# Expert feed-forward on one core: the weights become the stationary operand of the inner products, and the next tile's expert number is read ahead of the outer products

## What is computed

```
for _ in range(LOOPS):                      # 2
    z_norm = _rmsnorm(z, norm_w)
    logits = z_norm @ router_w
    scores = softmax(logits); topk_vals, topk_idx = top_k(scores, 2)
    topk_vals = topk_vals / (sum(topk_vals) + EPS)
    for e in range(E):                      # 8
        h = silu(flat_z @ w1[e]) * (flat_z @ w3[e])
        mixed = mixed + flat_cw[:, e:e + 1] * (h @ w2[e])
    z = z + mixed.reshape(B, S, D)
```

## Time and profile before

| what | value |
|---|---|
| median of three runs | 1051.33 us |
| the profiled execution | 1050.72 us, its span 1049.0 us |
| granted TensorE clock, mean | 0.989 |
| PE busy | 94% of the span |
| DVE, ACT, POOL busy | 66%, 55%, 55% |
| experts' stage | about 350 to 1028 us of the span |

### The profile page before, as it was taken

How to read it: one execution, slowest core, us unless ns; L and a number is a source line. 1 busy time by engine, 2 the same in 40 slices (tenths; PEclk the granted TensorE clock), 3 DMA queues, 4 the chain that set the end, 5 groups by cost and what they waited for, 6 DMA issues and landing times.

```text
span 1049.0 us, 22711 instructions
## 1 busy us (share of the span) xinstructions
PE 987.4 (94%) x7246; PEld 678.7 (65%) x7246; DVE 690.5 (66%) x1497; ACT 574.7 (55%) x1122; POOL 579.5 (55%) x755
## 2 busy tenths in 40 slices
PE   7999997989999899999999999999999999999991
PEld 5677776668888577665666765666755566666661
DVE  7889987999999454684435557535469433575557
ACT  4578786668888545433335565335574333333333
POOL 3356686866798755444443366443365544455435
PEclk9999999999999999999999999999999999999996
DMA  9921111000000234334346435338434433665573
GB/s 315 370 68 31 38 32 22 1 6 21 15 26 16 67 107 125 87 69 101 91 109 167 132 98 139 88 106 181 112 111 117 96 91 92 170 173 119 143 187 130
DMA packets 153818, 109.26 MB, mean 104 GB/s; under 512 B 100992, under 2 KB 140544, under 8 KB 153728
## 3 DMA queue, kind: packets, MB, share of 16 engines
q1 hardware_dynamic: 140096, 70.82, 26.5%
q0 software_dynamic: 13632, 37.24, 12.0%
HBM read 54.27 MB, written 31.20 MB: 81 GB/s over the span
## 4 chain that ended last, share of the span: by engine, by line
PE 69%; DVE 9%; POOL 7%; DMA 6%; ACT 4%; issue 3%; SPq 0%; another core or an unknown queue 0%; POOLq 0%; ACTq 0%; DVEq 0%
PE psum_s L930 32%; PE psum_o L2336 16%; PE psum_s L2325 6%; DMA arena<-arena 4%; PE psum_s L1758 3%; PE psum_t L1753 2%; PE psum_t L764 2%; PE psum_o L1804 2%; POOL arena L1057 2%; DVE arena L1489 1%; DMA arena<-in_rope 1%; PE psum_o L1799 1%; PE psum_o L1811 1%; PE psum_s L1735 1%; PE psum_t L2300 1%
## 5 line engine op out<-in xcount | busy, mean ns | idle before, releaser
L930 PE MATMUL psum_s<-w_all,arena 128*128 x1704 | 392.0, 380 | 4.6 <-issue 1.9
L1980 POOL DMA_INDIRECT token_rows<-arena,result_row_of_row x142 | 147.1, 1036 | 296.5 <-ACT arena L2089 291.2
L930 PEld LDWEIGHTS psum_s<-w_all,arena 128*128 128x128 f16 x1704 | 157.8, 98 | 185.2 <-issue 10.9
L2336 PE MATMUL psum_o<-w_all,arena 128*128 x1704 | 209.4, 273 | 9.1 <-DVE arena L2264 8.2
L915 DVE SCALAR_TENSOR_TENSOR arena<-psum_s,gate_scale,arena 128x512 f32<-128x512 f32 x142 | 106.5, 750 | 161.1 <-ACT arena L909 80.6
L2336 PEld LDWEIGHTS psum_o<-w_all,arena 128*128 128x128 f16 x1704 | 164.7, 98 | 54.1 <-issue 15.4
L2264 DVE TENSOR_TENSOR arena<-psum_s,arena 128x512 f16<-128x512 f32 x142 | 97.8, 689 | 132.3 <-ACT arena L2082 114.2
L2089 ACT ACTIVATE arena<-psum_o 128x256 f32<-128x256 f32 x142 | 54.3, 383 | 216.8 <-PE psum_o L2336 214.1
L891 POOL DMA_INDIRECT arena<-sorted_rows,token_of_row x142 | 139.9, 986 | 49.3 <-issue 40.2
L909 ACT ACTIVATE arena<-psum_s,silu_scale 128x512 f32<-128x512 f32 x142 | 97.6, 687 | 108.1 <-PE psum_s L930 56.6
L2082 ACT ACTIVATE arena<-psum_s 128x512 f16<-128x512 f32 x142 | 84.7, 597 | 33.1 <-PE psum_s L2325 22.9
(11 more groups left out here) (326 smaller groups left out, 1364.8 us busy)
## 6 DMA issues: line engine op xcount, KB each, us to landing
arena<-token_rows SPq DMA_DIRECT2D x64, 256.0 KB, 3.1
w_all<-in_L_ffn_w SPq DMA_DIRECT2D x24, 512.0 KB, 10.1
sorted_rows<-w_all SPq DMA_DIRECT2D x24, 256.0 KB
out<-x_sb SPq DMA_DIRECT2D x7, 512.0 KB, 3.1
arena<-arena SPq DMA_TRANSPOSE x172, 2.4
arena<-sorted_rows,token_of_row POOLq DMA_INDIRECT x142
token_rows<-arena,result_row_of_row POOLq DMA_INDIRECT x142
x_sb<-in_L_attn_x SPq DMA_DIRECT2D x1, 2048.0 KB, 14.8
```

Of the source, the lines that this page charges most:

```text
L930: last = nc.tensor.matmul(bank, e_xT[:, u, lx * DC + c, :], w_split[:, bass.ds(e * EW + at, FF)], start=(q == 0), stop=(q == 3 * DC - 1))
L1980: nc.gpsimd.indirect_dma_start(rows, bass.IndirectOffsetOnAxis(ap=targets[:, at : at + 1], axis=0), y_row[:, u, :], None).then_inc(s_sent[ ...
L2336: last = nc.tensor.matmul(psum_e, hT[:, lh, c, :], w_split[:, bass.ds(e * EW + at, D)], start=(q == 0), stop=(q == 3 * FC - 1))
```

## The change

Four things, all in the experts' stage:

1. `inner` exchanges the operands. The weights are stationary (blocks of 128x128, at a place held in a register) and the token rows move (128 columns). For each m there are now 4 blocks f of the hidden values times 6 products: 24 matmuls of 128 columns for each m, 48 for a tile. The result has the hidden values on the partitions, so `turn_h` and its semaphore are gone; `h_row` is now `h_all`, already turned, and `h_hi` and `h_lo` read it from SBUF instead of `psum_h`.
2. The addresses are worked out ahead of the matmuls: `place` adds a constant to a multiple of the expert's number, in bytes, once for each place (16 places for each m of `inner`, 8 for `outer`), and the operands use the registers as they are.
3. The waits: `inner(n, e, 0)` waits for `silu(n-1)`, `inner(n, e, 1)` for `gate(n-1)`, which `turn_h` did for both. `gate` waits on its own engine for `h_lo` of the tile before.
4. The number of the next tile's expert is read behind `beside` and ahead of `outer(n-1)`; at the end of a pass the wait for the next pass's numbers stands there too.

```diff
+        W_BASE, LAST_COLUMN = 16512, 2 * (P - 1)
...
+        w_bytes = w_all[:, :].bitcast(mybir.dt.uint8)
...
+            if s:
+                dve.wait_ge(s_h_lo, s)
-            nc.vector.scalar_tensor_tensor(h_row, psum_b, gate_scale[:, 0:1], silu_a, ALU.mult,
+            nc.vector.scalar_tensor_tensor(h_all, psum_b, gate_scale[:, 0:1], silu_a, ALU.mult,
...
+        def place(pe, e, at):
+            r = pe.alloc_register()
+            pe.reg_alu(r, e * (2 * EW), 2 * at + W_BASE, ALU.add)
+            return pe.snap(r, donate=True, min_val=2 * at + W_BASE, max_val=2 * at + W_BASE + 2 * EW * (NE - 1),
+                           guaranteed_mod_val=0, out_of_modulus=2)
+
+        def stationary(r):
+            return w_bytes[:, bass.ds(r - (W_BASE + LAST_COLUMN), 2 * P)].bitcast(F16)
+
+        def moving(r):
+            return w_bytes[:, bass.ds(r - W_BASE, 2 * D)].bitcast(F16)
+
         def inner(pe, n, e, m):
             u = n % UNROLL
+            places = [[place(pe, e, ((m * DC + c) * 2 + lw) * GROUP + f * P + P - 1) for c in range(DC) for lw in range(2)] for f in range(FC)]
             if m == 0:
                 pe.wait_ge(s_turned[u], 16 * (n // UNROLL + 1))
+                if n:
+                    pe.wait_ge(s_silu, n)
+            elif n:
+                pe.wait_ge(s_h, n)
...
-                last = nc.tensor.matmul(bank, e_xT[:, u, lx * DC + c, :], w_split[:, bass.ds(e * EW + at, FF)],
-                                        start=(q == 0), stop=(q == 3 * DC - 1))
+            for f in range(FC):
+                for q, (c, lx, lw) in enumerate([(c, a, w) for c in range(DC) for a, w in ((0, 0), (1, 0), (0, 1))]):
+                    last = nc.tensor.matmul(bank[:, f * P : (f + 1) * P], stationary(places[f][2 * c + lw]),
+                                            e_xT[:, u, lx * DC + c, :], start=(q == 0), stop=(q == 3 * DC - 1))
...
-                act.wait_ge(s_th, s + 1)
-                nc.scalar.activation(hT[:, 0, :, :].rearrange("p c t -> p (c t)"), psum_h, ACT.Copy).then_inc(s_h_hi, 1)
+                act.wait_ge(s_h, s + 1)
+                nc.scalar.activation(hT[:, 0, :, :].rearrange("p c t -> p (c t)"), h_all, ACT.Copy).then_inc(s_h_hi, 1)
...
-                nc.vector.tensor_tensor(hT[:, 1, :, :].rearrange("p c t -> p (c t)"), psum_h,
+                nc.vector.tensor_tensor(hT[:, 1, :, :].rearrange("p c t -> p (c t)"), h_all,
...
-            def turn_h(n):
...
             def outer(n, e):
+                per = GROUP // D
+                places = [[place(pe, e, ((2 * DC + c // per) * 2 + lw) * GROUP + c % per * D) for lw in range(2)] for c in range(FC)]
                 pe.wait_ge(s_h_lo, n + 1)
...
-            before_e = None
+            before_e, e = None, expert(pe, 0, 0)
...
-                    if n:
-                        turn_h(n - 1)
-                    e = expert(pe, k, t)
                     for m in range(2 if n else 0):
                         inner(pe, n, e, m)
                     if k < END:
                         beside(k, plan, t)
+                    next_e = None
+                    if t + 1 < PASS[k]:
+                        next_e = expert(pe, k, t + 1)
+                    elif n + 1 < ALL:
+                        pe.wait_ge(s_eid, k + 2)
+                        next_e = expert(pe, k + 1, 0)
                     if n:
                         outer(n - 1, before_e)
```

More of the change, by code:

```diff
@@ L796, in sandwich_kernel @@
         silu_a = take(FF)
-        h_row = take(FF)
+        h_all = take(FF)
         hT = take(2 * FF // 2).bitcast(F16).rearrange("p (l c t) -> p l c t", l=2, c=FC)
@@ L815, in sandwich_kernel @@
         psum_a, psum_b = psum_s[:, 0:FF], psum_s[:, 512 : 512 + FF]
-        psum_h = psum_s[:, 1024:1536]
         psum_e = psum_o[:, 0:D]
@@ L827, in sandwich_kernel @@
         s_h = sem("h_ready")
-        s_th = sem("h_turned")
         s_h_hi = sem("hT_hi")
@@ L920, in expert @@
             return pe.value_load(expert_of[0:1, at : at + 1], min_val=0, max_val=NE - 1)
+        def place(pe, e, at):
[7 more added lines that the diff above has]
+            return w_bytes[:, bass.ds(r - W_BASE, 2 * D)].bitcast(F16)
         def inner(pe, n, e, m):
             u = n % UNROLL
+            places = [[place(pe, e, ((m * DC + c) * 2 + lw) * GROUP + f * P + P - 1) for c in range(DC) for lw in range(2)] for f in range(FC)]
             if m == 0:
                 pe.wait_ge(s_turned[u], 16 * (n // UNROLL + 1))
+                if n:
+                    pe.wait_ge(s_silu, n)
+            elif n:
+                pe.wait_ge(s_h, n)
             bank, signal = ((psum_a, s_a), (psum_b, s_b))[m]
-            for q, (c, lx, lw) in enumerate([(c, a, w) for c in range(DC) for a, w in ((0, 0), (1, 0), (0, 1))]):
-                at = ((m * DC + c) * 2 + lw) * GROUP
-                last = nc.tensor.matmul(bank, e_xT[:, u, lx * DC + c, :], w_split[:, bass.ds(e * EW + at, FF)],
-                                        start=(q == 0), stop=(q == 3 * DC - 1))
+            for f in range(FC):
+                for q, (c, lx, lw) in enumerate([(c, a, w) for c in range(DC) for a, w in ((0, 0), (1, 0), (0, 1))]):
+                    last = nc.tensor.matmul(bank[:, f * P : (f + 1) * P], stationary(places[f][2 * c + lw]),
+                                            e_xT[:, u, lx * DC + c, :], start=(q == 0), stop=(q == 3 * DC - 1))
             last.then_inc(signal, 1)
@@ L2333, in outer @@
                 for q, (c, lh, lw) in enumerate([(c, a, w) for c in range(FC) for a, w in ((0, 0), (1, 0), (0, 1))]):
-                    per = GROUP // D
-                    at = ((2 * DC + c // per) * 2 + lw) * GROUP + c % per * D
-                    last = nc.tensor.matmul(psum_e, hT[:, lh, c, :], w_split[:, bass.ds(e * EW + at, D)],
+                    last = nc.tensor.matmul(psum_e, hT[:, lh, c, :], moving(places[c][lw]),
                                             start=(q == 0), stop=(q == 3 * FC - 1))
                 last.then_inc(s_e, 1)
-            before_e = None
+            before_e, e = None, expert(pe, 0, 0)
             for k, plan in enumerate(plans):
-                pe.wait_ge(s_eid, k + 1)
                 for t in range(PASS[k]):
                     n = FIRST[k] + t
-                    if n:
-                        turn_h(n - 1)
-                    e = expert(pe, k, t)
                     for m in range(2 if n else 0):
@@ L2355, in _ @@
                         beside_end(k, plan, t)
-                    before_e = e
-            turn_h(ALL - 1)
+                    before_e, e = e, next_e
             outer(ALL - 1, before_e)
```

## The result

The changed kernel took 1038.48 us (median of 4 runs, 1037.29 to 1039.50) against 1052.28 for the kernel before beside it; the ratio is 0.987, 95% interval 0.985 to 0.990. It is faster by 13.8 us. The time lies inside the range, but the gain is half of the 28 us forecast.

What follows compares the result with a forecast made beforehand. Plain tiles were taken as bound by what the PE array streams. Gains of 8.6 (24 tiles), 22 (92 plain tiles) and 0.6 (last tile), less 3 for neighbours, gave -28 us: 1051.3 to 1023 us, range 1006 to 1043.

Steps and rivals of the forecast that it cites:

- where PE waits for others: Step on tiles where PE idles for h_lo: about 14 late tiles gain nothing, neighbours lose 3 us, last tile saves 0.6.
- 24 tiles x 0.36 = 8.6: Term for the tiles with L2300 beside them: each gains the array's whole 0.36 us, 8.6 us together.
- The array: PE's streaming in a tile: transposes save 0.44 us, 48 inner matmuls at 56 ns cost 0.08 more; 4.35 becomes 3.99.
- every rival with a dearer load: Register-addressed weight loads take longer on the array; at 64 ns the gain is gone, 1051 to 1060 us; chance 0.04.
- the stall of 0.12 us: PE's sequencer in 92 plain tiles: takes 0.12 us off each tile's 0.36 gain, with a gap ahead of the outer products.
- which the sum counts at 0: Term for 12 tiles, together with about 14 late for h_lo: no gain in any of them.
- The load's new place: Expert-number load moved ahead of outer(n-1): passes only PE's queue; y_copy and the sending DMA have over 2 us to spare.
- `h_hi` from SBUF: h_hi on ScalarE reads SBUF instead of PSUM: counted as costing nothing, 0 to 0.03 us either way.
- Instruction fetch: PE's longer program: 33 more queue packets at 0.2 us stall would cost 7 us, giving 1030, inside the range.
- neighbours with 3 us in all: Tiles near the late ones, with nearly no slack, become late for h_lo: a loss of 3 us in all.
- still fits: Stretch from 906 to 941 us: VectorE's 3.6 us a tile is under the new tile's 3.99 us.
- VectorE and ScalarE become the bound: Rival: slack shrinks everywhere; routing tiles and those with L2300 or L662 gain nothing, 14 us gained, 1037; chance 0.13.

Runs made afterwards that it cites:

- e3: Changed kernel with every tile using expert 0's weights at fixed addresses, without number loads or register operations: 1024.75 us, ratio 0.974.
- f4: Changed kernel with both the fetch waiting for the second half of inner and expert 0 at fixed addresses: 1011.51 us, ratio 0.963.
- e2: Changed kernel with the expert's number read at the start of its own tile again, in front of inner: 1037.00 us, ratio 0.986.
- e1: Changed kernel with GpSimd waiting for the signal of inner's second half before issuing the fetch: 1024.51 us, ratio 0.976.
- g1: Kernel before with each 512-column inner matmul cut into four of 128, fixed addresses at expert 0: 1101.30 us (one run).
- e4: Kernel before with two small memsets on GpSimd ahead of each fetch, so it starts closer to inner's end: 1052.68 us, ratio 1.002.
- g3: Changed kernel with each fetch a plain transfer of 128 consecutive rows, issued at the same place, instead of an indirect one: 1012.39 us (one run).

## Why the prediction was right and wrong

The forecast had 28 us to gain and the change gave 13.8. What failed is the step on where PE waits for others, and with it the term "24 tiles x 0.36 = 8.6".

*The array: right.* 48 inner matmuls take 2.84 us with the tail of the last (220 ns by L949, of which 56 count): 2.68, as forecast. Register addresses cost the array nothing there: in e3, with fixed ones, the 48 take the same 2.84 us. At 56 ns a pair every rival with a dearer load is out. Of tiles 25 to 42 (72.5 us) one took 4.37 us, and the others 4.01 in the mean.

*The sequencer in plain tiles: the stall of 0.12 us was mostly not there.* It was my estimate, and no run shows it, nor how many operations one FUSED_REGOPS does. With fixed addresses (e3) a plain tile takes 3.99 us, with registers 3.99 to 4.07. Yet fixed addresses were worth 12 to 14 us of the whole (e3 and f4), about what the prediction had given the sequencer (92 x 0.12 = 11). A plain tile has only 0.02 to 0.03 us of that, so most of it lies elsewhere: this term was near by luck. The additions pass in eight FUSED_REGOPS a tile (1136 in 142 tiles), of 42 to 88 ns each, where the forecast has 8 with up to 85:

```profile
L926 PEldq FUSED_REGOPS  x1136: 42/74/88, 350.6 to 1009.6; - x190
```

In one plain tile after (500.95 to 503.29 us) the two ahead of the outer products pass in 0.17 us, the three ahead of m = 0 in 0.38 and the three ahead of m = 1 in 0.34, together 0.89; before, the eight of `outer` took 0.94 (from 500.64) and the eight of `inner` 0.93 (from 503.34), with pairs between them.

In the tiles with L664, which the sum counts at 0, registers cost about 0.3 us: 4.44 to 4.50 us against 4.19 in e3. That took nearly the whole gain there; before, one took 4.54 us (its outer products start at 662.30, the next ones at 666.84). With so little of the stall in plain tiles, the first group gained 0.33 us each where I had 0.24 for most of them.

*The load's new place*: nothing, by e2. *`h_hi` from SBUF*: 626 ns in the mean (L2101) against 597 from PSUM before (L2082), within the 0.03 us of the forecast. *Instruction fetch*: 88 packets, 32 more, but in the regular tiles from 480 to 560 us PE is idle for only 0.5 us.

*Where PE waits for others: this step failed.* It charged neighbours with 3 us in all, gave the 24 tiles with L2300 their whole 0.36 us, and said of the stretch from 906 to 941 us that 3.6 us of VectorE a tile "still fits". All that took for granted that VectorE and ScalarE learn of b and a when these are done, as they do in these tiles before. After, VectorE learns of b some 0.95 us later. In a plain tile that costs nothing: `h_lo` ends at 523.87 + 0.69 = 524.56, 3.1 us after b ended, as forecast, since `h_hi` stands behind `y_copy` anyway. But VectorE's free time between gate and `h_lo` is 0.70 us instead of the 1.51 of e1, and where routing or statistics must fit into it, they don't. The same eight tiles after and in e1 (us, busy PE, PEld, DVE, ACT, POOL, clock, DMA, GB/s):

```profile
896.64:932.14 35.50, 33.24 (x484) 30.85 (x481) 28.71 (x65) 12.88 (x24) 17.58 (x16) 1.00 0.76 179
```

```profile
880.43:912.80 32.37, 32.19 (x483) 30.87 (x481) 28.73 (x69) 12.72 (x24) 17.15 (x16) 1.00 0.93 197
```

VectorE's work is 28.7 us in both, as before. With the signal late it does not fit (35.50 us), with the signal on time it does (32.37, the forecast 3.99 a tile plus 0.06). The argument was sound and its input was not.

The 24 tiles with L2300 (L2319 after) took 133.2 us before and 132.8 after, a gain of 0.4 us where the sum has 8.6. In e1 they took 125.3, a gain of 7.9. Here it is chiefly a, to ScalarE, that is late, with L766 waiting for it; e1 frees a and b together, so the share of each is not measured. This is the largest single miss of the sum.

The size nearly closes: the forecast gain was 28 us, the change gave 13.8, and with the one wait of e1 it is 26.2. That it closes so well is partly luck: the first group gained more than I gave it, and the 33 routing tiles lost 1 us even in e1, where I had at most 14 of them at nothing and the others gaining.

*The rivals.* "VectorE and ScalarE become the bound" (1037) came closest to the time. Its place was right, its reason only in part. In the routing tiles it holds in part: PE's wait for `h_lo` rose from 8.2 to 22.1 us and stays at 22.5 in e1, and even there they take 163.1 us against 162.1 before, so the shorter tile took their slack. In the tiles with L2300 and in those of the statistics it was the late signals.

*What in the profile of before could have warned.* GpSimd issues an indirect transfer for 0.97 us of each tile shortly before b ends. And the effect itself is there, in a few tiles: at the end of the first pass GpSimd issued four indirect transfers in a row, and a, with matmuls of 512 columns, ended at 471.45 + 5 x 0.216 + 0.38 = 472.91 while `silu` started 1.74 us later.

```profile
468.79 0.98 POOL L891 DMA_INDIRECT arena<-sorted_rows,token_of_row  x1 [0.30 <-issue]
...
470.07 0.97 POOL L891 DMA_INDIRECT arena<-sorted_rows,token_of_row  x1 [0.30 <-issue]
...
471.35 0.95 POOL L891 DMA_INDIRECT arena<-sorted_rows,token_of_row  x1 [0.30 <-issue]
...
471.45 2.76 PE L930 MATMUL psum_s<-w_all,arena 128*128 x12
...
472.60 0.99 POOL L1980 DMA_INDIRECT token_rows<-arena,result_row_of_row  x1 [0.30 <-issue]
...
474.65 0.69 ACT L909 ACTIVATE arena<-psum_s,silu_scale 128x512 f32<-128x512 f32 x1 [2.43 <-remote]
```

The record of a's signal stands at 474.63. The same happened at 819.5 us (1.69 late), and in three tiles of the first pass. I did not look for it; I took the hand-over of a and b as unchanged because no line of it was changed.

## What to carry to other kernels

A change in the shape of an engine's work can move the moment at which others learn of it; so bound the hand-over, not only the work. After such a change, compare for each signal the end of the last instruction with the start of the first one that waits for it, and sort the late ones by what the other engines were doing. When an experiment's time fits a theory, look at the row that the theory speaks of before you believe it: e3 had the right time for the wrong reason. And look at every signal of the engine, not only at the one that first caught the eye: in the tiles with L2319 it was a that was late.

## What the hardware showed that was not expected

- A signal of TensorE came late (by 0.96 us in the median after, by 0.56 in the tile of g1 above) when it stood at the end of a run of 128-column matmuls, 56 ns each, and GpSimd had begun to issue an indirect transfer 0.3 to 1.6 us earlier: 81 of 84 tiles after, 73 of 73 in g1. In most of these the transfer was the second of two that started about 1.3 us apart. With 512-column matmuls (216 ns) it was 0 of 88 in e4. Behind a plain transfer that started 0.97 us before b ended it was on time (g3: 2 of 127 late, both behind the indirect send).
- The width is not the whole of it. The outer products' signal (256 columns, 109 ns each) was late in 2 of 99 such tiles of e1, but there the transfer nearly always stood alone; behind a second transfer that started less than 1.6 us after the first it was late in 5 of 6 tiles after and in 10 of 11 in e3, and in none of 4 before, where the matmuls ahead of the outer products are long. And behind three or four indirect transfers in a row a signal behind 512-column matmuls came 1.7 us late in the kernel before (472.91 and 819.5 us).
- The array went on meanwhile: the outer products followed b at once and signalled in time (521.36 and 522.87 above, where b ended at 521.44). The record of b's signal is late (522.40) and the next matmuls are not, so the array did not stand still. What the signal waits for, no run here shows. Nor does one tell whether the lateness would be there without the profiler's records, of which PE makes nearly four times as many a microsecond at 56 ns as at 216.
- Register addresses and the loads of the expert's number cost little in a plain tile (0 to 0.08 us), but 13 us of the whole by the medians (e1 and f4).
